# A graph layer on one core: table blocks loaded into buffers that are free earlier, and the final normalisation one turn later

## The reference

```python
def ssp(v):
    return jax.nn.softplus(v) - jnp.log(2.0)
h = x @ W_in2f
Wij = ssp(f_ij @ W_filt1 + b_filt1) @ W_filt2 + b_filt2
Wij = Wij * rcut_ij[:, None]
x_ij = h[idx_j] * Wij
agg = jax.ops.segment_sum(x_ij, idx_i, num_segments=n_atoms)
out = ssp(agg @ W_out1 + b_out1) @ W_out2 + b_out2
return layernorm(x + out)
```

## Time and profile before

| | |
|---|---|
| median of 3 runs | 2133.01 us (2132.39 to 2133.57) |
| profiled execution | 2138.0 us, its span 2136.2 us |
| PE busy | 2010.7 us, 94% of the span |
| DVE busy | 1957.4 us, 92% |
| POOL busy | 1695.9 us, 79% |
| ACT busy | 1586.3 us, 74% |
| last product of the main part | begins 2045.45 us after the span's start |

### The profile page before, as it was taken

One profiled execution on the slowest core, in us unless ns is written; L12 is line 12 of the kernel. 1 busy time (PEld: TensorE's weight loads), 2 busy tenths in 40 slices (PEclk: granted clock), 3 DMA queues, 4 the chain that ended last, 5 costly groups with the idle time before them and its releaser, 6 DMA issues.

```text
span 2136.2 us, 53343 instructions
## 1 busy us (share of the span) xinstructions
PE 2010.7 (94%) x16433; PEld 1700.0 (80%) x16433; DVE 1957.4 (92%) x4022; ACT 1586.3 (74%) x3852; POOL 1695.9 (79%) x1051
## 2 busy tenths in 40 slices
PE   2589999999999999999999999999999999999946
PEld 2478888888888888888888888888888888888723
DVE  5579999999999999999999999999999999999837
ACT  1278788788787787887887878778878878778517
POOL 2358888888888888888888888888888888888854
PEclk8789999999999999999999999999999999999979
DMA  8546666665666566666666665666666666655574
GB/s 321 224 91 99 105 96 96 102 103 98 99 98 104 90 99 104 100 94 104 99 99 97 98 104 92 97 103 100 96 102 100 98 98 98 103 90 84 97 196 128
DMA packets 346340, 235.27 MB, mean 110 GB/s; under 512 B 86087, under 2 KB 325554, under 8 KB 345850
## 3 DMA queue, kind: packets, MB, share of 16 engines
q0 software_dynamic: 140976, 64.22, 32.6%
q1 hardware_dynamic: 194598, 150.79, 26.8%
q10 hardware_dynamic: 10476, 16.77, 2.1%
HBM read 145.44 MB, written 86.20 MB: 108 GB/s over the span
## 4 chain that ended last, share of the span: by engine, by line
PE 65%; DMA 13%; POOL 7%; issue 7%; DVE 4%; ACT 2%; SPq 1%; POOLq 0%; DVEq 0%; ACTq 0%
PE unit_psum L1739 18%; PE unit_psum L1759 15%; PE both_psum L1695 12%; DMA table<-total,index 11%; PE total_psum L1708 8%; POOL table L789 7%; PE pre_psum L1676 6%; PE both_psum L1720 4%; PE both_psum L1691 2%; DMA x_t<-in_x_t 1%; DMA src_g<-in_src 1%; ACT out_rows L1083 1%; DVE route_hot L1377 1%; DVE scat_hot L1391 0%; DVE acc_t L1406 0%
## 5 line engine op out<-in xcount | busy, mean ns | idle before, releaser
L789 POOL DMA_INDIRECT table<-total,index x979 | 1614.7, 1649 | 334.3 <-issue 237.6
L1739 PE MATMUL unit_psum<-moving,route_hot 128*128 128x258 f32 x4088 | 637.3, 295 | 3.1 <-DVE acc_t L1406 2.1
L1739 PEld LDWEIGHTS unit_psum<-moving,route_hot 128*128 128x128 f32 x4088 | 526.2, 190 | 48.7 <-ACT ring L961 32.7
L1391 DVE TENSOR_SCALAR scat_hot<-node_iota,ring 128x448 fp32r<-128x448 uint16 x1022 | 479.7, 482 | 17.5 <-PE unit_psum L1759 13.1
L939 ACT ACTIVATE h_dst<-both_psum,edge_cols 128x128 f32<-128x128 f32 x1564 | 446.1, 379 | 49.0 <-PE both_psum L1720 48.6
L961 ACT ACTIVATE ring<-unit_psum 128x258 fp32r<-128x258 f32 x1022 | 370.5, 403 | 150.1 <-PE unit_psum L1739 136.2
L1759 PE MATMUL unit_psum<-scat_hot,ring 64*128 64x448 f32 x4088 | 461.1, 372 | 11.2 <-DVE acc_t L1406 9.7
L1759 PEld LDWEIGHTS unit_psum<-scat_hot,ring 64*128 64x128 f32 x4088 | 377.4, 186 | 88.1 <-ACT ring L961 37.8
L1695 PE MATMUL both_psum<-w_f,hidden 128*128 128x128 f32 x3128 | 422.1, 278 | 0.0
L1377 DVE TENSOR_SCALAR route_hot<-node_iota,slot_cols 128x896 fp32r<-128x896 uint16 x584 | 403.9, 725 | 1.8 <-PE unit_psum L1739 1.6
L1695 PEld LDWEIGHTS both_psum<-w_f,hidden 128*128 128x128 f32 x3128 | 398.5, 192 | 5.5
(11 more groups left out here) (125 smaller groups left out, 1575.1 us busy)
## 6 DMA issues: line engine op xcount, KB each, us to landing
dst_b<-dst SPq DMA_DIRECT2D x391, 128.0 KB, 3.3
src_b<-src SPq DMA_DIRECT2D x245, 128.0 KB
f_t<-in_f_t SPq DMA_DIRECT2D x98, 256.0 KB
table<-total,index POOLq DMA_INDIRECT x979
table<-zeros ACTq DMA_DIRECT2D x20, 640.0 KB, 9.9
window<-h_parts SPq DMA_DIRECT2D x391, 32.0 KB, 2.0
parts<-table SPq DMA_DIRECT2D x48, 256.0 KB, 5.2
h_parts<-h_out SPq DMA_DIRECT2D x12, 384.0 KB, 6.7
```

Of the source, the lines that this page charges most:

```text
L789: pool.indirect_dma_start(tables[k], bass.IndirectOffsetOnAxis(index[:, i, k:k + 1], 0), total[:, i, k, 0:DIM], None, compute_op=ALU.add). ...
L1391: dve.tensor_scalar(scat_hot[:, (n - 1) % HOTS, :], node_iota[:, 0:BUCKET], ring[:, RING_AT[r[1], slot_tile(s)], 2 * DIM:2 * DIM + 1].bitc ...
L1739: last = pe.matmul(unit_psum[:, k % 2, 0:MOVING], route_hot[:, tile, k * P:(k + 1) * P], moving[:, tile, :], start=(tile == 0), stop=(tile ...
```

## The change

Three buffers of `parts` now lie over `f_t` (features), `same` (masks) and `message`, and only the fourth (`parts_last`) lies over the ring. SP's main part ends with a wait for the last product that reads `same` and `message` in place of the one for the last sum from the ring; the first load waits for the last first-layer product (which reads `f_t`), and the load of chunk 3 for the transposes of chunk 0. In the last layers shift and scaled rows are made at distance i - 3 in place of i - 2, their inputs have three buffers in place of two, and exponential and logarithm now come ahead of the scaled rows and the copy on ACT, and the clamp ahead of the shift on DVE.

```diff
-        stats = sb("stats", [P, 2, 4, 6], F32)
+        stats = sb("stats", [P, 3, 4, 6], F32)
...
-        y_rows = at(52320, "y_rows", [P, 2, CHUNK], F32)
-        parts = at(4096, "parts", [P, PARTS, TABLES, CHUNK], F32)
+        y_rows = at(56512, "y_rows", [P, 3, CHUNK], F32)
+        parts_last = at(4096, "parts_last", [P, TABLES, CHUNK], F32)
+        parts = [f_t[:, 0:TABLES, :], same[:, :, :, :].rearrange("p b k e -> p b (k e)"),
+                 message[:, :, :, :].rearrange("p b k a -> p (b k a)")[:, 0:TABLES * CHUNK]
+                 .rearrange("p (k n) -> p k n", k=TABLES), parts_last[:, :, :]]
...
-                sp.wait_ge(taken_done, TAKEN_BEFORE[STEPS])
+                sp.wait_ge(total_mm_done, through((0, GROUPS - 1), plain))
...
                 previous(sp, e_half, c, summed, PARTS)
+                if is_at(c, 0):
+                    sp.wait_ge(pre_done, PAIRS)
+                if is_at(c, PARTS - 1):
+                    sp.wait_ge(e_agg_t, 1)
```

On ACT, in `last_layers`:

```diff
-                c = plus(i, -2)
+                c = i
                 if is_chunk(c):
-                    b, tiles = c[1] % 2, tiles_of(c)
+                    b, n = c[1] % 2, tiles_of(c) * P
+                    act.wait_ge(e_clamp, after_chunk(c))
+                    act.activation(soft[:, b, 0:n], soft[:, b, 0:n], ACT.Exp).then_inc(e_exp, 1)
+                    act.wait_ge(e_exp, after_chunk(c))
+                    act.activation(soft[:, b, 0:n], soft[:, b, 0:n], ACT.Ln, bias=1.0).then_inc(e_ln, 1)
+                c = plus(i, -3)
+                if is_chunk(c):
+                    b, y, tiles = c[1] % 2, c[1] % 3, tiles_of(c)
                     act.wait_ge(e_shift, after_chunk(c))
                     previous(act, out_stored[b], c, landed_chunk)
                     for k in range(tiles):
                         d = slice(k * DIM, (k + 1) * DIM)
-                        last = act.activation(out_rows[:, b, d], y_rows[:, b, d], ACT.Identity,
+                        last = act.activation(out_rows[:, b, d], y_rows[:, y, d], ACT.Identity,
...
                 c = plus(i, 1)
                 if is_chunk(c):
...
                     act.activation(agg_t[:, b, 0:n], both_psum[:, b, 0:n], ACT.Copy).then_inc(e_agg_sb, 1)
-                if is_chunk(plus(i, -2)):
-                    store_rows(plus(i, -2))
-                c = i
-                if is_chunk(c):
-                    b, n = c[1] % 2, tiles_of(c) * P
-                    act.wait_ge(e_clamp, after_chunk(c))
-                    act.activation(soft[:, b, 0:n], soft[:, b, 0:n], ACT.Exp).then_inc(e_exp, 1)
-                    act.wait_ge(e_exp, after_chunk(c))
-                    act.activation(soft[:, b, 0:n], soft[:, b, 0:n], ACT.Ln, bias=1.0).then_inc(e_ln, 1)
-
+                if is_chunk(plus(i, -3)):
+                    store_rows(plus(i, -3))
```

On DVE, in `last_layers`:

```diff
-                c = plus(i, -2)
-                if is_chunk(c):
-                    b, tiles = c[1] % 2, tiles_of(c)
-                    dve.wait_ge(e_inv, after_chunk(c))
-                    previous(dve, e_norm, c, after_chunk)
-                    dve.scalar_tensor_tensor(norm_shift[:, b, 0:tiles], mean_var[:, b, 0:tiles, 0], -1.0,
-                                             inv_dev[:, b, 0:tiles], ALU.mult, ALU.mult).then_inc(e_shift, 1)
-
                 c = i
...
+                c = plus(i, -3)
+                if is_chunk(c):
+                    y, tiles = c[1] % 3, tiles_of(c)
+                    dve.wait_ge(e_inv, after_chunk(c))
+                    previous(dve, e_norm, c, after_chunk, 3)
+                    dve.scalar_tensor_tensor(norm_shift[:, y, 0:tiles], mean_var[:, y, 0:tiles, 0], -1.0,
+                                             inv_dev[:, y, 0:tiles], ALU.mult, ALU.mult).then_inc(e_shift, 1)
```

More of the change, by code:

```diff
@@ L379, in build @@
         x_rows = nc.alloc_sbuf_tensor_at("x_rows", [P, NODE_ROWS // P * DIM], F32, offset=x_rows_at)
-        stats = sb("stats", [P, 2, 4, 6], F32)
-        mean_var = sb("mean_var", [P, 2, 4, 2], F32)
-        ln_var = sb("ln_var", [P, 2, 4], F32)
-        inv_dev = sb("inv_dev", [P, 2, 4], F32)
+        stats = sb("stats", [P, 3, 4, 6], F32)
+        mean_var = sb("mean_var", [P, 3, 4, 2], F32)
+        ln_var = sb("ln_var", [P, 3, 4], F32)
+        inv_dev = sb("inv_dev", [P, 3, 4], F32)
         eps_col = sb("eps_col", [P, 1], F32)
@@ L725, in load_tables @@
                 previous(sp, e_half, c, summed, PARTS)
+                if is_at(c, 0):
+                    sp.wait_ge(pre_done, PAIRS)
+                if is_at(c, PARTS - 1):
+                    sp.wait_ge(e_agg_t, 1)
                 for k in range(TABLES):
-                    sp.dma_start(parts[:, b, k, 0:tiles * DIM].rearrange("p (t d) -> p t d", d=DIM),
+                    sp.dma_start(parts[b][:, k, 0:tiles * DIM].rearrange("p (t d) -> p t d", d=DIM),
                                  tables[k][bass.ds(chunk_number(c) * CHUNK, tiles * P), :]
@@ L829, in last_layers @@
                     for k in range(1, TABLES):
-                        before = parts[:, q, 0, 0:n] if k == 1 else half_sum[:, b, 0:n]
+                        before = parts[q][:, 0, 0:n] if k == 1 else half_sum[:, b, 0:n]
                         if k > 1:
                             pool.wait_ge(e_half, ADDS * c[1] + k - 1)
-                        pool.tensor_tensor(half_sum[:, b, 0:n], before, parts[:, q, k, 0:n], ALU.add).then_inc(e_half, 1)
+                        pool.tensor_tensor(half_sum[:, b, 0:n], before, parts[q][:, k, 0:n], ALU.add).then_inc(e_half, 1)
             run_last_layers(pool, last_layers)
@@ L1091, in last_layers @@
                     act.activation(agg_t[:, b, 0:n], both_psum[:, b, 0:n], ACT.Copy).then_inc(e_agg_sb, 1)
[L1092 to L1100 removed]
+                if is_chunk(plus(i, -3)):
+                    store_rows(plus(i, -3))
                 c = plus(i, -1)
                 if is_chunk(c):
[L1104 removed]
+                    y, tiles = c[1] % 3, tiles_of(c)
                     act.wait_ge(e_aggr, after_chunk(c))
[L1106 to L1107 removed]
+                    previous(act, e_inv, c, after_chunk, 3)
+                    act.activation(ln_var[:, y, 0:tiles], mean_var[:, y, 0:tiles, 1], ACT.Ln, bias=eps_col[:, 0:1]
                                    ).then_inc(e_ln_var, 1)
                     act.wait_ge(e_ln_var, after_chunk(c))
[L1110 to L1111 removed]
+                    previous(act, e_norm, c, after_chunk, 3)
+                    act.activation(inv_dev[:, y, 0:tiles], ln_var[:, y, 0:tiles], ACT.Exp, scale=-0.5
                                    ).then_inc(e_inv, 1)
@@ L1591, in last_layers @@
                     for k in range(tiles):
-                        last = dve.bn_stats(stats[:, b, k, :], y_rows[:, b, k * DIM:(k + 1) * DIM])
+                        last = dve.bn_stats(stats[:, y, k, :], y_rows[:, y, k * DIM:(k + 1) * DIM])
                     last.then_inc(e_stats, 1)
@@ L1596, in last_layers @@
                     for k in range(tiles):
-                        last = dve.bn_aggr(mean_var[:, b, k, :], stats[:, b, k, :])
+                        last = dve.bn_aggr(mean_var[:, y, k, :], stats[:, y, k, :])
                     last.then_inc(e_aggr, 1)
```

12 lines of the change are left out of this document (6 added, 6 removed).

## The result

The changed kernel takes 2148.91 us (median of 4 executions, 2146.86 to 2150.31) against 2132.70 us (2132.30 to 2133.57). The ratio is 1.0071 with a 95% interval of 1.0058 to 1.0085, so it is slower by 0.7%. 2145.6 us was forecast, in a range of 2137.0 to 2150.5 us.

The account below looks back on a forecast made before the run. The loads set the start of the last layers, and a loop through hidden, shift and ACT's work closed each turn. Terms -7.0 + 10.1 + 3.0 + 6.5 = +12.6 us on the median 2133.01 gave 2145.6 us, range 2137 to 2150.5.

Parts of the forecast that it names:

- part 1: End of SP's main part: the wait for the ring's last sum goes, so the first load starts earlier, -7.0 us.
- part 2: On SP, chunk 3's load now waits for the transposes of chunk 0: cost 0, at most 0.7 us.
- A late block of chunk 3: Sign against the forecast: a late table block of chunk 3 showing in the waits; no size given.
- part 3: ACT's turns, with copy, pair and clamp in line: three of 4.64 us, nine of 6.20 us, +10.1 us.
- part 5: TensorE in the last layers: clock drops behind idle gaps, 4 of 9 turns 1.63 us longer, +6.5 us.
- alternation: In the last layers, turns with a slow and a fast pair were expected to alternate, 4 of 9 slow.
- part 4: ACT from chunk 12's exponential to its scaled rows: 7.9 us in place of 4.96, +3.0 us.
- A: Rival: the last layers' loop holds and TensorE's clock stays at 2.4 GHz; +6.1 us, 2139.1 us; chance 0.27.
- B: Rival: in the last layers the pair finds its copy made, turns about 4.30 us; 2122.9 us; chance 0.06.
- C: Rival: leaving the main part or another wait takes the 7.0 us of earlier start; 2152.6 us; chance 0.05.
- D: Rival: no change, last-layer turns of 4.8 to 5.5 us because parts of the loop overlap; chance 0.07.

Follow-up runs that it names:

- the run with the fourth free buffer: The changed kernel with the fourth table-block buffer over the scattered rows' buffer, so chunk 3's load waits for no transposes; ratio 1.0066 to the kernel before.
- the filled kernel: The changed kernel with eight unread extra products on TensorE behind the second products, from turn 3 on; median 2142.01 us, ratio 1.0032 to the kernel before.
- the run with the copy first: The changed kernel with ScalarE's copy of chunk i + 1 moved ahead of the exponential of chunk i; median 2122.46 us, ratio 0.9930 to the kernel before.

## Why the prediction was right

- **The early start** (part 1) was -7.04 us forecast and is -6.92 measured against the last product, and the jump still takes 2.65 us to the first load. The run with the loads alone gives its full gain.
- **Chunk 3's wait** (part 2) was 0 with 0.7 us at most. GpSimd waited 0.41 us for that block, and the run without the wait shows no change. A late block of chunk 3 was one of the signs by which the prediction would be wrong: it showed, and cost nothing, since the copy of that chunk came later still.
- **The turn in line** (part 3) was 4.64 and 6.20 us and is 4.64 and 6.17. The loop was named step by step, and moving the copy alone took it away.
- **The clock** (part 5) was four long turns of nine at 1.63 us each. Four were long in the profile, by 1.40 to 1.80 us, 6.1 us in all. Filling TensorE's idle time took them all away. What the prediction called alternation is a rough picture: two long turns followed each other, and two short ones did. That the count came out exactly is in part luck, since three were long in the run with the fourth free buffer. What the forecast left out is the clock in the last turn (0.5 us) and at the end. The Trainium skill (TensorE: Matmul & The Clock Gate, section "Why this matters for your kernels") has the rule by which gaps as short as these leave the clock high. It did not hold here: behind gaps of 2.39 to 2.64 us the clock was at 0.50 in four turns, while behind others of 2.64 and 2.96 us it was at 1.00.
- **The end** (part 4) is the step that was off: 3.0 us forecast, 4.06 measured. The prediction said that ScalarE would be busy throughout. It did nothing for 1.68 us ahead of the deviation of chunk 11, of which the store is 0.5 (as in the 0.51 us elsewhere) and the rest a wait for the variance of that chunk, because the second products of that chunk fell into a stretch at 1.2 GHz:

```profile
2135.30 1.92 PE L1915 MATMUL total_psum<-w_o,hidden 128*128 128x128 f32 x8
```

They took 1.92 us, against 1.05 at the high clock. With the clock kept, the end took 8.00 us against the 7.9 worked out.
- **First load to first addition** had no term and gave 1.10 us. That the sum came out within 0.1 us (+12.52 against +12.6) is luck to this extent: this 1.10 us and the 1.06 us by which the end was off cancel.
- **The median** is 3.3 us above the forecast, although the sum of the end came out 0.1 us from it. The profiled execution before was 5.3 us longer than the median of its kernel (2138.0 against 2132.70), and that of the changed kernel 0.8 us (2149.68 against 2148.91). The prediction added a difference of one profile to a median and had no term for this. The last product of the main part begins up to 9.5 us apart in the twelve profiled executions, so the main part can make such a difference; that it did so here is not shown, since the other executions have no trace.
- **The rivals.** A (the same loop, the clock kept) is the filled kernel: 2142.01 us, 7.4 above the kernel before beside it, of which 1.4 is its slow first turn, against the +6.1 worked out. B is the run with the copy first. C falls with the first load at 2041.90, and D with turns of 6.17 us at the high clock.

## What to carry to other kernels

In a hand-written pipeline over several engines, walk the loop through every in-order queue before moving a block: from an instruction to what it releases, and back to the same instruction one turn later. A producer that is moved behind a consumer of an earlier chunk may now stand behind a consumer of its own chunk, and then everything between lies in line; here this turned turns of 4.8 to 5.3 us into 6.2 though no engine had more to do. And a longer turn can cost a second time, if TensorE then idles so much in each that it loses its clock, as in four of the eight full turns here.

## What was not expected of the hardware

- From the first load to the first addition it took 7.36 us before and 8.43 us in the run with the new layers alone, the two kernels with the loads behind the last product; in the ten others it took 6.06 to 7.10 us. In the first two the loads began after the DMA engines had been nearly idle for the last 10.0 and 6.9 us (mean shares of 0.01 and 0.02); in the changed kernel it was the last 3.2 us (0.01), and about as long in the nine others. Whether it is that, the buffers' place or the time was not tried.
- The last product of the same main part began between 2036.0 and 2045.5 us in the twelve profiled executions, and the first load of the kernels that do not wait for it came 0.8 to 4.2 us ahead of it. What varies there stays open.
